# A first layer's preparation put in another order: grouped bias units and a convolution shared by two engines

## The chip, the cores and the metric

The kernel runs on one core of a Trainium2 chip. The metric is the device time of one execution in microseconds; several executions are made and their median is compared. The profile is one execution, read by engine: PE is TensorE (PEld its weight loads), DVE is VectorE, ACT is ScalarE, POOL is GpSimd, SP is the engine that issues most loads. All data are fp32.

## The reference, cut to what matters

The program is a chain of layers. Only the first, a convolutional attention with offsets learned from the queries, is touched:

```python
xn = bn(x)                                        # x: (2, 128, 32, 32)
q = gconv1x1(xn, qw)                              # 8 groups of 16 channels
off = conv(q by group, off_dw_w, stride 4, pad 1) # depthwise 6x6, output 8x8
off = tanh(off_pw_w . gelu(off + b)) * 4          # two offsets for each of 64 keys
vgrid = (grid + off) scaled to [-1, 1]
kv = grid_sample(xn by group, vgrid)              # bilinear
k, v = gconv1x1(kv, kw), gconv1x1(kv, vw)
pos = grid_q[:, :, None] - vgrid[:, None]         # 1024 queries x 64 keys x (x, y)
bias = sign(pos) * log1p(abs(pos))
bias = relu(bias @ cpb_w1 + cpb_b1)               # 2 -> 32
bias = relu(bias @ cpb_w2 + cpb_b2)               # 32 -> 32
bias = bias @ cpb_w3 + cpb_b3
attn = softmax(q k^T * scale + bias);  out = attn v
```

Since pos is a difference along x and one along y, the first bias layer is a sum of a part that depends on the query's column (A) and one that depends on its row (B). After the first layer come two more attention layers, a trajectory network, a gated linear attention and experts; they are the same in both kernels.

## The kernel before

`l0_bias` (L222) runs one block of all engines: `l0_prepare` (L235) and behind it `l0_scores` (L517). Each engine has its own program, in the written order, and engines meet only at semaphores, so an instruction that waits holds all behind it on its engine. PSUM has eight banks of 128x512 fp32.

`l0_prepare` goes through these steps. x is normalised in two halves, the first by VectorE (L289), the second by ScalarE (L351). Four projections by TensorE give the queries (L418), which ScalarE puts into an image with a border (`qpad`, L356) and VectorE copies flat (L296). The depthwise convolution is 36 products of TensorE with diagonal weights that VectorE builds (`TAP`, L292), each over every fourth pixel (L424). Gelu (L359), a product (L432) and Tanh (L362) give the offsets; TensorE meanwhile transposes the image (L438) and ScalarE evicts it (`XT`, L365). VectorE turns offsets into positions (L300 to L306): `spread` feeds a product with ones that gives every sampling point's coordinates (L447), and `pos` goes through Abs, Sign and Ln on ScalarE (L374 to L377) and becomes `F` (L308) and its negative `NF` (L309).

Then come 16 bias units, one for each image and head, of which each is two matmuls of 32 rows (L467, one for A, one for B), and each pair of banks is evicted by VectorE, the last few in part by ScalarE (L315, L322, L392, L399). Between them stand eight sampling steps: ScalarE makes a hat function in two operations (L383, L386), POOL multiplies it with the other axis' (`wt`, L280) and TensorE sums (L476). Keys and values follow (L492, L493), then their spreading by head (`vm`, `KM`) and eight transposes (L499).

`l0_scores` first multiplies B by the second layer (`offsets`, L644), evicts that as `NEGC` by both engines (L559, L589), computes `constants` (L654, L592) and then runs 64 cycles. In a cycle half of the hidden units go POOL (row sum, L553), ScalarE (relu, L567), TensorE (L673), ScalarE (L573), TensorE (L711); the other half go VectorE (a maximum of A and of a negated B, `max1`, L605), TensorE (L673), VectorE (`max2`, L613), TensorE (L720). The negated B for `max1` is a product of `NF` (`negb`, L666), made once for four cycles; every four cycles a tile of scores is evicted (L620) and a query-key product opens the next (L701).

SP loads the packed weights of the layer in two parts and the next stage's behind them (L2557, L2558, L2546); x is loaded by ScalarE's queue (L348).

Of the kernel before, what the change touches and what calls it, by code (L numbers as in the profile page):

```python
# [19 lines left out]
P = 128  # L20
NB = 2
# [125 lines left out]
def l0_pack(w):  # L147
# [37 lines left out]
    p.add("tmask", (rows[:, None] % 4 == np.arange(4)).astype(np.float32))  # L185
# [5 lines left out]
    p.add("qgrid", np.tile(cq.reshape(1, HW), (P, 1)))  # L191
# [16 lines left out]
UNITS = NB * HEADS  # L208
LOOPED = 12
WITH_SAMPLE = (2, 1, 2, 1, 1, 1, 1, 1)  # L210
A_ON_ACT = (11, 12, 13, 14, 15)
B_ON_ACT = (14, 15)


def unit(u):

    return u % NB, u // NB


def evicted(on_act, u, act):  # L220

    return sum((k in on_act) == act for k in range(u + 1))  # L222


def l0_bias(nc, X, PS, W, first, rest, loads, KM, VT, Q, A, WORK, NF, SALL, x_in, x_dram):
# [12 lines left out]
def l0_prepare(st, block, X, PS, W, first, rest, KM, VT, Q, A, WORK, NF, x_in, x_dram):
    sb, sem = st.sb, st.sem
    B = WORK[:, 0:NB * PAIRS * PIX].rearrange("p (r n i x) -> p r n i x", r=2, n=NB * PAIRS, i=4)  # L240
    SPARE = WORK[:, NB * PAIRS * PIX:]
# [4 lines left out]
    TAP = part(4096, TAPS * P).rearrange("p (t o) -> p t o", o=P)  # L246
    qpad = part(9216, NB * PADW * PADW).rearrange("p (b y x) -> p b y x", b=NB, x=PADW)
# [15 lines left out]
    F = sb("l0_f", [P, HALF])  # L263

    inner = lambda b, y0, n: qpad[:, b, 1 + y0:1 + y0 + n, 1:1 + HW]
    flat2 = lambda v: v.rearrange("p a n -> p (a n)")
    CONV, ZED, GRID_X, GRID_Y, SAMPLE, KVB = 4, 5, 6, 4, 6, 7
    
    

    @block.gpsimd
    def _(pool):
        pool.memset(qpad[:], 0.0).then_inc(sem("border"), 1)
        pool.memset(ones[:], 1.0).then_inc(sem("ones"), 1)
        pool.wait_ge(sem("hx"), 1)
        for c in range(8):
            pool.wait_ge(sem("hy"), c + 1)
            if c >= 2:
                pool.wait_ge(sem("sampled"), c - 1)
            pool.tensor_tensor(wt[:, c % 2], hx[:], hy[:, c % 2], ALU.mult).then_inc(sem("wt"), 1)  # L280

    @block.vector
    def _(dve):
        link = Chain(dve, sem("dve_chain"))
        dve.wait_ge(first, 16)
        link(dve.tensor_scalar(s1[:], W["bn1_g"], BN_SCALE, None, ALU.mult))
        dve.sem_inc(sem("s1"), 1)
        dve.wait_ge(x_in[0], 16)
        dve.tensor_scalar(XN[:, 0:PIX], X[:, 0:PIX], s1[:, 0:1], W["bn1_b"], ALU.mult, ALU.add).then_inc(sem("xn0"), 1)  # L289
        for h in range(2):  # L290
            t = slice(h * TAPS // 2, (h + 1) * TAPS // 2)
            dve.tensor_tensor(TAP[:, t], bc(W["ident"], 1, TAPS // 2), bc(W["off_dw_w"][:, t], 2, P), ALU.mult  # L292
                              ).then_inc(sem("taps"), 1)
        for n in range(NCH):
            dve.wait_ge(sem("q_in"), n + 1)
            dve.tensor_copy(Q[:, n * CH:(n + 1) * CH], PS[:, n]).then_inc(sem("q_flat"), 1)  # L296

        dve.wait_ge(rest, 16)
        dve.wait_ge(sem("tanh"), 1)
        link(dve.scalar_tensor_tensor(V[:], V[:], 4.0, W["kgrid"], ALU.mult, ALU.add))  # L300
        link(dve.tensor_scalar(V[:], V[:], 2.0 / 7.0, -1.0, ALU.mult, ALU.add))
        link(dve.tensor_scalar(px[:], V[:], 1.0, HW / 2.0, ALU.add, ALU.mult))
        dve.tensor_tensor(spread[:], bc(px[:], 1, HEADS), bc(W["first"], 2, KEYS), ALU.mult).then_inc(sem("spread"), 1)
        link(dve.tensor_tensor(sel[:], V[:].rearrange("p (t k) -> p t k", t=4), bc(W["tmask"], 2, 16), ALU.mult))
        link(dve.tensor_reduce(own[:], sel[:].rearrange("p t k -> p k t"), AX.X, ALU.add))
        dve.tensor_tensor(pos[:], bc(W["qgrid"], 1, 16), bc(own[:], 2, HW), ALU.subtract).then_inc(sem("pos"), 1)  # L306
        dve.wait_ge(sem("logs"), 1)
        dve.tensor_tensor(F[:], sgn[:], mag[:], ALU.mult).then_inc(sem("f"), 1)  # L308
        dve.scalar_tensor_tensor(NF[:], sgn[:], -1.0, mag[:], ALU.mult, ALU.mult)  # L309

        def a_out(u):
            b, g = unit(u)
            n = b * HEADS + g
            dve.wait_ge(sem("ab"), u + 1)
            dve.tensor_scalar(A[:, n // 2, (n % 2) * 16:(n % 2) * 16 + 16].rearrange("p u q -> p (u q)"),  # L315
                              PS[:, 2 * b], W["cpb_b1"], None, ALU.add).then_inc(sem("a_dve"), 1)

        def b_out(u):
            b, g = unit(u)
            n = b * HEADS + g  # L320
            dve.wait_ge(sem("ab"), u + 1)
            dve.tensor_copy(B[:, :, n // 2, 2 * (n % 2):2 * (n % 2) + 2].rearrange("p r i x -> p i r x"),  # L322
                            PS[:, 2 * b + 1].rearrange("p (i r x) -> p i r x", i=2, r=2)).then_inc(sem("b_dve"), 1)

        for u in range(LOOPED):
            if u not in A_ON_ACT:
                a_out(u)
            b_out(u)
        dve.wait_ge(sem("sampled"), 8)
        got = PS[:, SAMPLE:SAMPLE + NB, 0:P].rearrange("p b (g k) -> p b g k", g=2)  # L330
        link(dve.tensor_scalar(kv[:], got[:, :, 0], W["pmask"][:, 0:1], None, ALU.mult))
        dve.scalar_tensor_tensor(kv[:], got[:, :, 1], W["pmask"][:, 1:2], kv[:], ALU.mult, ALU.add).then_inc(sem("kv"), 1)
        b_out(LOOPED)
        dve.wait_ge(sem("k"), 1)
        for b in range(NB):
            m = bc(W["gmask"], 2, KEYS)
            dve.tensor_tensor(vm[:, b], bc(PS[:, KVB, NB * KEYS + b * KEYS:NB * KEYS + (b + 1) * KEYS], 1, HEADS), m,
                              ALU.mult).then_inc(sem("vm"), 1)
        for b in range(NB):
            m = bc(W["gmask"], 2, KEYS)  # L340
            dve.scalar_tensor_tensor(KM[:, b], bc(PS[:, KVB, b * KEYS:(b + 1) * KEYS], 1, HEADS), DH ** -0.5, m,
                                     ALU.mult, ALU.mult).then_inc(sem("km"), 1)
        b_out(LOOPED + 1)

    @block.scalar
    def _(act):
        for b in range(NB):
            act.dma_start(X[:, b * PIX:(b + 1) * PIX], x_dram[b].rearrange("c h w -> c (h w)")).then_inc(x_in[b], 16)  # L348
        act.wait_ge(sem("s1"), 1)
        act.wait_ge(x_in[1], 16)  # L350
        act.activation(XN[:, PIX:T], X[:, PIX:T], ACT.Identity, bias=W["bn1_b"], scale=s1[:, 0:1]  # L351
                       ).then_inc(sem("xn1"), 1)
        act.wait_ge(sem("border"), 1)
        for n in range(NCH):
            act.wait_ge(sem("q"), n + 1)
            act.activation(inner(n // 2, 16 * (n % 2), 16), PS[:, n].rearrange("p (y x) -> p y x", x=HW),  # L356
                           ACT.Copy).then_inc(sem("q_in"), 1)
        act.wait_ge(sem("conv"), 1)
        act.activation(off[:].rearrange("p b k -> p (b k)"), PS[:, CONV, 0:NB * KEYS], ACT.Gelu,  # L359
# [3 lines left out]
        for n in range(4):  # L363
            act.wait_ge(sem("xt"), n + 1)
            act.activation(XT[:, 4 * n:4 * n + 4].rearrange("p c k -> p (c k)"), PS[:, n],  # L365
                           ACT.Copy).then_inc(sem("xt_out"), 1)
        act.wait_ge(rest, 16)
        act.wait_ge(sem("grid"), 1)
        act.activation(hy[:, 0], flat2(PS[:, GRID_X:GRID_X + 2]), ACT.Abs, bias=W["minus_x"]).then_inc(sem("ax"), 1)
        act.wait_ge(sem("ax"), 1)  # L370
        act.activation(hx[:], hy[:, 0], ACT.Relu, bias=1.0, scale=-1.0).then_inc(sem("hx"), 1)
# [5 lines left out]
        act.activation(mag[:], mag[:], ACT.Ln, bias=1.0).then_inc(sem("logs"), 1)  # L377
        act.wait_ge(sem("hx"), 1)

        def hat(c):  # L380
            if c >= 2:
                act.wait_ge(sem("wt"), c - 1)
            act.activation(hy[:, c % 2], flat2(PS[:, GRID_Y:GRID_Y + 2]), ACT.Abs, bias=W["minus_y"][:, c:c + 1]  # L383
                           ).then_inc(sem("ay"), 1)
            act.wait_ge(sem("ay"), c + 1)
            act.activation(hy[:, c % 2], hy[:, c % 2], ACT.Relu, bias=1.0, scale=-1.0).then_inc(sem("hy"), 1)  # L386

        def a_out(u):
            b, g = unit(u)
            n = b * HEADS + g  # L390
            act.wait_ge(sem("ab"), u + 1)
            act.activation(A[:, n // 2, (n % 2) * 16:(n % 2) * 16 + 16].rearrange("p u q -> p (u q)"),  # L392
                           PS[:, 2 * b], ACT.Identity, bias=W["cpb_b1"]).then_inc(sem("a_act"), 1)

        def b_out(u):
            b, g = unit(u)
            n = b * HEADS + g
            act.wait_ge(sem("ab"), u + 1)
            act.activation(B[:, :, n // 2, 2 * (n % 2):2 * (n % 2) + 2].rearrange("p r i x -> p i r x"),  # L399
                           PS[:, 2 * b + 1].rearrange("p (i r x) -> p i r x", i=2, r=2), ACT.Copy  # L400
                           ).then_inc(sem("b_act"), 1)

        for c in range(8):
            hat(c)
        for u in range(LOOPED - 1, UNITS):
            a_out(u)
            if u in B_ON_ACT:
                b_out(u)
# [2236 lines left out]
```

## Time and profile before

| what | us |
|---|---|
| median of 3 runs (1671.84 to 1678.54) | 1673.09 |
| profiled execution, its own time | 1676.29 |
| its span, first to last instruction | 1674.4 |
| PE busy / DVE busy / ACT busy / POOL busy | 1500.5 / 886.2 / 872.5 / 320.8 |
| first product of the score loop, from the span's start | 89.90 |
| mean granted TensorE clock over the span | 0.955 |

A timeline row gives the start, the duration, the engine, the line, the operation, what it writes and reads, the shapes and the count; in brackets stands how long the engine had been idle and who released it. A row with a count is several instructions merged. The granted clock is a share of the full 2.4 GHz; its two levels are 1.0 and 0.5. The column holds 1.00 until the first recorded change.

### The profile page before, as it was taken

To read this page: it belongs to the slowest core of one execution; us is meant where nothing else is said; L and a number is where in the kernel's file an instruction comes from. 1 tells how busy PE (TensorE), PEld (TensorE's weight loads), DVE (VectorE), ACT (ScalarE), POOL (GpSimd) and SP (SyncE) were. 2 spreads that over 40 slices of the span, in tenths; PEclk is the share of its full clock that TensorE was granted. 3 is DMA by queue.
4 is the path that set the end of the run, shared out by engine and by line. 5 is a ranking of instruction groups with operands and counts; after the bars stand their busy time and mean duration, and the time that the engine had idled before them with its cause. 6 is when DMAs were issued, how large, how long until landed. Compare 5 with 4: busy or idle time off the path is not lost. (4 is left out here: it accounts for less than half of the span.)

```text
span 1674.4 us, 29793 instructions
## 1 busy us (share of the span) xinstructions
PE 1500.5 (90%) x12334; PEld 739.5 (44%) x12334; DVE 886.2 (53%) x1364; ACT 872.5 (52%) x1292; POOL 320.8 (19%) x139
## 2 busy tenths in 40 slices
PE   6889999999778997999999999899999999939678
PEld 4322222222243774666666666554444444316333
DVE  2578888888772554677777777110002000258243
ACT  3567777777543435677777776232222222250451
POOL 0746666666220001000000000000000000020000
PEclk9589999999998999799999999899999999979899
DMA  1000000000001003444344431000000000000000
GB/s 65 1 2 2 2 2 2 2 2 2 2 22 77 0 1 118 147 150 162 134 173 177 165 151 39 1 1 0 1 0 0 0 0 0 31 0 4 1 1 25
DMA packets 21089, 69.66 MB, mean 42 GB/s; under 512 B 736, under 2 KB 17248, under 8 KB 18656
## 3 DMA queue, kind: packets, MB, share of 16 engines
q1 hardware_dynamic: 20672, 66.76, 10.7%
q8 instruction: 96, 1.57, 0.4%
q10 hardware_dynamic: 288, 1.05, 0.2%
q14 instruction: 33, 0.27, 0.1%
HBM read 33.21 MB, written 34.60 MB: 40 GB/s over the span
## 5 line engine op out<-in xcount | busy, mean ns | idle before, releaser
L553 POOL TENSOR_TENSOR l_work<-l_a_scores,l_work 128x2048 f32<-128x2048 f32 x64 | 232.9, 3640 | 126.5 <-PE banks L673 126.5
L1909 PE MATMUL banks<-s_h,pack_l2f_l3f 128*128 128x512 f32 x512 | 221.0, 592 | 0.0
L1938 ACT ACTIVATE s_h<-banks,pack_l2f_l3f 128x512 f32<-128x512 f32 x128 | 88.0, 688 | 239.2 <-PE banks L1909 175.7
L1510 ACT ACTIVATE r_e<-banks,r_max 128x512 f32<-128x512 f32 x256 | 162.1, 685 | 51.2 <-DVE r_max L1551 51.1
L613 DVE TENSOR_TENSOR l_work<-banks,sc_negc 128x1024 f32<-128x1024 f32 x128 | 156.2, 1221 | 49.6 <-PE banks L720 33.2
L573 ACT ACTIVATE l_work<-banks,pack_l 128x1024 f32<-128x1024 f32 x128 | 142.7, 1115 | 74.7 <-PE banks L673 73.7
L673 PE MATMUL banks<-l_work,pack_l 32*32 32x512 f32 x4096 | 159.6, 606 | 23.5 <-ACT l_work L573 19.8
L1545 DVE TENSOR_REDUCE r_raw<-banks 128x1 f32<-128x640 f32 (+1 forms) x128 | 109.8, 858 | 90.6 <-PE banks L1435 88.9
L1455 PE MATMUL banks<-pack_l2a,r_e 128*128 128x128 f32 x1024 | 147.5, 285 | 10.4 <-ACT r_e L1510 10.2
L1909 PEld LDWEIGHTS banks<-s_h,pack_l2f_l3f 128*128 128x128 f32 x512 | 97.3, 190 | 122.5 <-issue 122.5
L1435 PE MATMUL banks<-r_k,r_q 32*128 32x128 f32 (+3 forms) x832 | 148.8, 466 | 1.1 <-DVE r_v L1379 1.1
L605 DVE TENSOR_TENSOR l_work<-banks,l_a_scores 128x2048 f32<-128x2048 f32 x64 | 146.0, 2281 | 0.7 <-PE banks L666 0.7
L567 ACT ACTIVATE l_work<-l_work 128x1024 f32<-128x1024 f32 x128 | 134.3, 1052 | 9.6 <-POOL l_work L553 9.6
L1455 PEld LDWEIGHTS banks<-pack_l2a,r_e 128*128 128x128 f32 x1024 | 112.0, 142 | 54.7 <-ACT r_e L1510 46.1
L1964 DVE TENSOR_SCALAR s_k<-banks,pack_l2f_l3f 128x512 f32<-128x512 f32 x12 | 9.0, 750 | 221.8 <-PE banks L1914 221.8
L1435 PEld LDWEIGHTS banks<-r_k,r_q 32*128 32x128 f32 x832 | 87.4, 188 | 71.7 <-issue 55.0
L673 PEld LDWEIGHTS banks<-l_work,pack_l 32*32 32x32 f32 x4096 | 42.1, 103 | 138.2 <-issue 103.3
L2136 POOL MEMSET ga_keep<- 128x1024 f32 x1 | 1.0, 951 | 474.0 <-SPq L2067 474.0
L1559 DVE COPY r_pt<-banks 128x512 f32<-128x512 f32 x128 | 87.9, 687 | 4.1 <-PE banks L1455 3.5
L1518 ACT ACTIVATE r_pt<-banks 128x512 f32<-128x512 f32 x128 | 76.5, 597 | 25.1 <-PE banks L1455 25.1
L1420 PE MATMUL banks<-pack_l2a,r_q 32*128 32x257 f32 x224 | 80.1, 437 | 0.0
L1551 DVE CUSTOM_DVE_ANT_0 banks<-banks,r_band,r_raw 128x384 f32<-128x384 f32 (+1 forms) x128 | 75.9, 593 | 6.3 <-DVE r_raw L1545 0.2
(399 smaller groups left out, 2079.1 us busy)
## 6 DMA issues: line engine op xcount, KB each, us to landing
distances<-r_rd SPq DMA_DIRECT2D x16, 2048.0 KB, 6.5
r_band<-distances SPq DMA_DIRECT2D x16, 1536.0 KB, 7.0
pack_l2f_l3f<-pack_dram_l2f SPq DMA_DIRECT2D x1, 2244.5 KB, 10.4
pack_l2f_l3f<-pack_dram_l3f SPq DMA_DIRECT2D x1, 1248.5 KB, 7.0
residual<-x ACTq DMA_DIRECT2D x2, 512.0 KB, 6.1
out<-residual SPq DMA_DIRECT2D x4, 256.0 KB, 2.0
pack_l<-pack_dram_l SPq DMA_DIRECT2D x1, 945.0 KB, 7.5
pack_l2a<-pack_dram_l2a SPq DMA_DIRECT2D x1, 715.0 KB, 5.5
```

The costliest lines, as they stand in the source:

```text
L553: pool.tensor_tensor(image(H1R[:, (c + 1) % 3]), bc(a, 2, 16), bc(b, 3, HW), ALU.add).then_inc(sem("added"), 1)
L567: act.activation(h, h, ACT.Relu).then_inc(sem("relu"), 1)
L573: act.activation(H2R[:, (2 * c + part) % 3], PS[:, RELU:RELU + 2], ACT.Relu, bias=W["cpb_b2"]).then_inc(sem("h2_relu"), 1)
L605: dve.tensor_tensor(image(H1M[:, c % 2]), bc(b, 3, HW), bc(a, 2, 16), ALU.max).then_inc(sem("h1_max"), 1)
L613: dve.tensor_tensor(image(H2M[:, (2 * c + part) % 3]), image(PS[:, MAX + j:MAX + j + 2]), bc(NEGC[:, j:j + 2, n, i, rows(half)], 3, HW), A ...
L673: ins = pe.matmul(PS[32 * u:32 * u + 32, bank], w2(j), h[32 * j:32 * j + 32, u], start=True, stop=True, tile_position=(32 * j, 32 * u))
L1435: ins = pe.matmul(PS[:, 2 * (t % 2) + a, col:col + n * P], Qm[at, a, h % 2, b * PIX + t * P:b * PIX + (t + 1) * P], K[at, a, b, slot:slot ...
L1455: ins = pe.transpose(PS[:, 4 + h, j * P:(j + 1) * P], E[:, t % 2, c:c + P], W["ident"])
L1510: act.activation(E[:, t % 2, a * CH:(a + 1) * CH], PS[:, 2 * (t % 2) + a], ACT.Exp, bias=mx[:, t % 2:t % 2 + 1], scale=-1.0).then_inc(sem( ...
L1545: dve.tensor_reduce(raw[:, one], v[:, lo:hi], AX.X, ALU.min).then_inc(sem("far"), 1)
L1909: ins = pe.matmul(bank, W["w2"][:, col:col + P], H1[:, c, m], start=(m == 0), stop=(m == HB - 1))
L1938: act.activation(H[:, c, k], PS[:, g % 8], ACT.Tanh, bias=bias).then_inc(sem("tanh"), 1)
```

## The change

The preparation is written anew; the score loop keeps its order with small edits.

- Loads: SP waits for x before it sends the second part of the weights and the next stage's.
- Both halves of x are normalised by VectorE. TensorE starts with five products on a constant that nobody reads. The first half of the transposes moves ahead of the convolution.
- The convolution is split: 12 taps stay on TensorE, 24 go to VectorE in two alternating accumulators, whose sum a last product of TensorE with the identity adds. The bordered image has another layout, so that a tap is one access pattern.
- `pos` comes before `spread`; the table for Ln is loaded explicitly behind Tanh; Abs, Sign and Ln come before the sampling coordinates on ScalarE. TensorE waits for `hx` before the first unit.
- The signs of the y rows of half the keys are folded into `tmask` and `qgrid`, so `NF` is gone.
- The 16 units become eight groups: four matmuls on all four row groups, into banks 0 to 3. VectorE evicts both images' A in one instruction, ScalarE both images' B. A group waits for both evictions of the one before.
- Sampling: three of eight weights stay on ScalarE and POOL, five are made by VectorE from ScalarE's distance. The order is written out. The sampled sums share bank 6 or 7 with keys and values.
- The first row sum on POOL moves between its second and third product.
- The offsets' products and the evictions to `NEGC` (halved, by image) move into the preparation, between keys and values. `constants` moves into the first cycle of the loop; `negb` serves eight cycles instead of four.

```diff
-    p.add("tmask", (rows[:, None] % 4 == np.arange(4)).astype(np.float32))
+    turned = (rows[:, None] >= P // 2) & (np.arange(16) // 4 % 2 == 1)
+    sign = np.where(turned, np.float32(-1.0), np.float32(1.0))
+    p.add("tmask", (rows[:, None] % 4 == np.arange(4)).astype(np.float32)[:, :, None] * sign[:, None, :])
...
+PE_TAPS = 12
+ON_POOL = (0, 2, 4)
+ON_DVE = (1, 3, 5, 7, 6)
+UNIT_ORDER = ("u0", "u1", "s1", "u2", "s0", "u3", "s3", "u4", "s2", "u5", "s5", "u6", "s4", "u7", "s7", "s6")
...
     @block.gpsimd
...
+        for c in ON_POOL:
+            pool.wait_ge(sem("hat"), c // 2 + 1)
+            if c:
+                pool.wait_ge(sem("sampled"), SAMPLE_ORDER.index(c - 2) + 1)
+            pool.tensor_tensor(wt[:, 0], hx[:], hy[:, 0], ALU.mult).then_inc(sem("wt_pool"), 1)
+            if c == 2:
...
+                rows_sum(pool, A, B, H1R, 0).then_inc(sem("added"), 1)
     @block.vector
...
+        dve.wait_ge(sem("q_in"), NCH)
+        for t in range(PE_TAPS, TAPS):
+            k, n = t % 2, (t - PE_TAPS) // 2
...
+            if n:
+                dve.wait_ge(chain, n)
+                ins = dve.scalar_tensor_tensor(ACCS[:, k], tap(t), weight, ACCS[:, k], ALU.mult, ALU.add)
+            else:
+                ins = dve.tensor_scalar(ACCS[:, k], tap(t), weight, None, ALU.mult)
+            ins.then_inc(chain, 1)
...
+        def a_out(g):
+            dve.wait_ge(sem("ab"), g + 1)
+            n, t = g // 2, g % 2 * 16
+            dve.tensor_scalar(A[:, n::PAIRS, t:t + 16].rearrange("p b u x -> p b (u x)"), PS[:, 0:NB], W["cpb_b1"], None,
+                              ALU.add).then_inc(sem("a"), 1)
+        def weights(c):
...
+            dve.tensor_scalar(wt[:, slot], hy[:, slot], -1.0, 1.0, ALU.mult, ALU.add).then_inc(sem("near"), 1)
...
+            dve.scalar_tensor_tensor(wt[:, slot], wt[:, slot], 0.0, hx[:], ALU.max, ALU.mult).then_inc(sem("wt_dve"), 1)
+        for k in range(4):
+            a_out(2 * k)
+            weights(2 * k + 1)
+            a_out(2 * k + 1)
+        weights(6)
...
     @block.scalar
...
+        act.preload_act_table_set("natural_log_exp_and_others")
...
+        for k in range(4):
+            distance(2 * k + 1)
+            b_out(2 * k)
+            distance(2 * k)
+            if 2 * k in ON_POOL:
+                hat(2 * k)
+            b_out(2 * k + 1)
...
     @block.tensor
...
+        pe.wait_ge(sem("busy"), 1)
+        for _ in range(5):
+            keep_clock(busy[:, 0:P], busy)
...
+        for t in range(PE_TAPS):
+            pe.matmul(PS[:, CONV, 0:NB * KEYS], TAP[:, t], tap(t), start=(t == 0), stop=False)
+        pe.wait_ge(sem("conv_dve"), 1)
...
+        pe.wait_ge(sem("hx"), 1)
+        def units(g):
+            if g == 0:
+                pe.wait_ge(sem("f"), 1)
+                pe.wait_ge(sem("xt_dve"), 2)
+            else:
+                pe.wait_ge(sem("a"), g)
+                pe.wait_ge(sem("b"), g)
             for c in range(2):
...
+                for b in range(NB):
+                    r = 32 * (NB * c + b)
...
+                    ins = pe.matmul(PS[:, NB * c + b], W["cpb_w1"][r:r + 32, g * P:(g + 1) * P], f, start=True, stop=True,
+                                    tile_position=(r, 0))
...
+        row_offsets(pe, PS, W, B, 0).then_inc(sem("c"), 1)
         pe.wait_ge(sem("kv"), 1)
...
+        row_offsets(pe, PS, W, B, 1).then_inc(sem("c"), 1)
...
 def l0_scores
...
+            if c == 0:
+                constants()
+            if c % 8 == 7 and c + 1 < CYCLES:
+                negb((c + 1) // 8)
...
             def load_l0(sp):
                 sp.dma_start(tile[:, 0:split], packs["l0"][:, 0:split]).then_inc(arrived["l0"], 16)
+                for b in range(NB):
+                    sp.wait_ge(x_in[b], 16)
                 sp.dma_start(tile[:, split:], packs["l0"][:, split:]).then_inc(rest, 16)
```

## Rows read from the trace of the kernel before

**Rows 1.** Stages: stretch, length, busy us (count) by engine, clock, DMA share, GB/s.

```profile
32.62:42.62 10.00, 3.36 (x33) 2.26 (x33) 3.14 (x9) 8.56 (x13) 0.00 (x0) 0.79 0.01 2
42.62:80.12 37.50, 34.05 (x196) 12.68 (x196) 20.33 (x33) 19.50 (x21) 29.51 (x11) 0.55 0.00 0
80.12:89.90 9.78, 7.57 (x109) 4.21 (x108) 2.78 (x2) 7.29 (x9) 0.00 (x0) 0.86 0.01 3
89.90:118.74 28.84, 25.25 (x367) 6.14 (x382) 21.82 (x14) 18.58 (x19) 14.56 (x4) 0.82 0.01 2
```

**Rows 2.** Timeline up to 35 us: start, duration, engine, line, operation, count, [idle, releaser].

```profile
5.17 0.81 DVE L289 TENSOR_SCALAR l_work<-residual,l_s,pack_l 128x1024 f32<-128x1024 f32 x1 [0.15 <-DMA residual<-x]
...
5.90 5.02 DVE L292 TENSOR_TENSOR l_work<-pack_l 128x2304 f32<-128x2304 f32 x2
...
8.99 1.28 ACT L351 ACT_TABLE_LOAD   x1 [8.99 <-DMA residual<-x]
...
11.57 3.47 PE L418 MATMUL banks<-l_work,pack_l 128*128 128x512 f32 x4 [1.76 <-ACT l_work L351]
...
15.73 16.89 PE L424 MATMUL banks<-l_work 128*128 128x128 f32 x72 [0.69 <-ACT l_work L356]
...
33.42 1.97 PE L438 MATMUL banks<-pack_l,l_work 128*128 128x128 f32 x16
```

**Rows 3.** Timeline from the convolution's end to the first units.

```profile
33.89 0.23 DVE L300 SCALAR_TENSOR_TENSOR l_v<-l_v,pack_l 128x64 f32<-128x64 f32 x1 [17.48 <-ACT l_v L362]
...
35.40 1.14 PE L447 MATMUL banks<-l_spread,l_ones 32*128 32x512 f32 x8
...
35.77 0.69 DVE L306 TENSOR_TENSOR l_pos<-pack_l,l_own 128x512 f32<-128x512 f32 x1
...
41.21 0.63 ACT L377 ACTIVATE l_mag<-l_mag 128x512 f32<-128x512 f32 x1
...
42.62 2.09 PE L467 MATMUL banks<-l_f,pack_l 32*128 32x512 f32 x8 [6.08 <-DVE l_f L308]
```

**Rows 4.** Timeline in the unit stage and at the offsets.

```profile
44.74 0.75 DVE L315 TENSOR_SCALAR l_a_scores<-banks,pack_l 128x512 f32<-128x512 f32 x1 [1.57 <-PE banks L467]
...
50.51 2.08 PE L467 MATMUL banks<-l_f,pack_l 32*128 32x512 f32 x4
...
52.52 1.08 PE L476 MATMUL banks<-l_wt,l_work 128*32 128x128 f32 x16
...
53.13 1.11 ACT L383 ACTIVATE l_hy<-banks,pack_l 128x1024 f32<-128x1024 f32 x1 [2.15 <-POOL l_wt L280]
...
53.78 2.35 POOL L280 TENSOR_TENSOR l_wt<-l_hx,l_hy 128x1024 f32<-128x1024 f32 x1 [0.68 <-PE banks L476]
...
82.02 2.75 PE L644 MATMUL banks<-l_work,pack_l 32*32 32x512 f32 x64
```

**Rows 5.** Timeline in the score loop, at its entry and around one L666.

```profile
100.63 2.28 DVE L605 TENSOR_TENSOR l_work<-banks,l_a_scores 128x2048 f32<-128x2048 f32 x1
...
108.21 2.28 DVE L605 TENSOR_TENSOR l_work<-banks,l_a_scores 128x2048 f32<-128x2048 f32 x1
...
118.74 2.28 DVE L605 TENSOR_TENSOR l_work<-banks,l_a_scores 128x2048 f32<-128x2048 f32 x1
...
238.81 2.28 DVE L605 TENSOR_TENSOR l_work<-banks,l_a_scores 128x2048 f32<-128x2048 f32 x1
...
242.35 1.12 PE L666 MATMUL banks<-l_nf,pack_l 32*128 32x256 f32 x4
...
243.66 2.28 DVE L605 TENSOR_TENSOR l_work<-banks,l_a_scores 128x2048 f32<-128x2048 f32 x1
...
245.64 3.64 POOL L553 TENSOR_TENSOR l_work<-l_a_scores,l_work 128x2048 f32<-128x2048 f32 x1 [2.19 <-PE banks L673]
...
246.69 1.23 DVE L613 TENSOR_TENSOR l_work<-banks,sc_negc 128x1024 f32<-128x1024 f32 x1 [0.75 <-PE banks L720]
...
249.40 2.28 DVE L605 TENSOR_TENSOR l_work<-banks,l_a_scores 128x2048 f32<-128x2048 f32 x1
```

More of the change, by code:

```diff
@@ L205, in mlp_pack, with l0_bias @@
     return p
[L208 to L225, printed above, removed]
+PE_TAPS = 12
+ON_POOL = (0, 2, 4)
+ON_DVE = (1, 3, 5, 7, 6)
+CYCLES = NB * PAIRS * 2 * 4
+RING = NB * PAIRS * 4 * P
+UNIT_ORDER = ("u0", "u1", "s1", "u2", "s0", "u3", "s3", "u4", "s2", "u5", "s5", "u6", "s4", "u7", "s7", "s6")
+SAMPLE_ORDER = tuple(int(x[1]) for x in UNIT_ORDER if x[0] == "s")
+def l0_bias(nc, X, PS, W, first, rest, loads, KM, VT, Q, A, WORK, F, SALL, x_in, x_dram):
     with ExitStack() as ctx:
         st = Stage(nc, ctx)
+        NEGC = st.sb("sc_negc", [P, 4, NB * PAIRS, 4, HW])
+        negb2 = st.sb("sc_negb2", [P, 1])
         block = st.block()
@@ L303, in _ @@
         dve.tensor_tensor(spread[:], bc(px[:], 1, HEADS), bc(W["first"], 2, KEYS), ALU.mult).then_inc(sem("spread"), 1)
-        link(dve.tensor_tensor(sel[:], V[:].rearrange("p (t k) -> p t k", t=4), bc(W["tmask"], 2, 16), ALU.mult))
-        link(dve.tensor_reduce(own[:], sel[:].rearrange("p t k -> p k t"), AX.X, ALU.add))
-        dve.tensor_tensor(pos[:], bc(W["qgrid"], 1, 16), bc(own[:], 2, HW), ALU.subtract).then_inc(sem("pos"), 1)
+        for n in range(2, 4):
+            dve.wait_ge(sem("xt"), n + 1)
+            dve.tensor_copy(turned(n), PS[:, XT_BANK[n]]).then_inc(sem("xt_dve"), 1)
@@ L388, in a_out @@
[L388 to L408, printed above, removed]
+        act.wait_ge(rest, 16)
+        act.wait_ge(sem("grid"), 1)
+        act.activation(hy[:, 0], flat2(PS[:, GRID_X:GRID_X + 2]), ACT.Abs, bias=W["minus_x"]).then_inc(sem("ax"), 1)
+        act.wait_ge(sem("ax"), 1)
+        act.activation(hx[:], hy[:, 0], ACT.Relu, bias=1.0, scale=-1.0).then_inc(sem("hx"), 1)
+        act.wait_ge(sem("hx"), 1)
@@ new lines, in distance @@
+        def distance(c):
+            slot = c % 2
+            if slot and c >= 3:
+                act.wait_ge(sem("near"), ON_DVE.index(c - 2) + 1)
+            elif c >= 2:
+                act.wait_ge(sem("wt_pool"), c // 2)
+            act.activation(hy[:, slot], flat2(PS[:, GRID_Y:GRID_Y + 2]), ACT.Abs, bias=W["minus_y"][:, c:c + 1]
+                           ).then_inc(sem("far_odd" if slot else "far_even"), 1)
+        def hat(c):
+            act.wait_ge(sem("far_even"), c // 2 + 1)
+            act.activation(hy[:, 0], hy[:, 0], ACT.Relu, bias=1.0, scale=-1.0).then_inc(sem("hat"), 1)
@@ L666, in negb @@
                 ins = pe.matmul(PS[:, NEGB, low * 256:low * 256 + 256], W["cpb_w1"][r:r + 32, k * P:(k + 1) * P],
-                                NF[r:r + 32].rearrange("p (k y) -> p k y", y=HW)[:, :, rows(half)], start=True,
+                                F[r:r + 32].rearrange("p (i r x) -> p i r x", i=2, r=2)[:, :, 1], start=True,
                                 stop=True, tile_position=(r, 0), skip_group_check=True)
@@ L744, in _, with reg_wait @@
         layer3_max(CYCLES - 1)
+def reg_wait(eng, sem, value, passed):
+    eng.wait_ge(sem, value)
+    eng.sem_inc(passed, 1)
 def l0_attend(nc, X, PS, W, SALL, VT, loads):
```

346 lines of the change are left out of this document (161 added, 185 removed).

## The prediction

> **What bounds the kernel now.** I read the stage table first: the first layer's preparation, from the start to the first product of the score loop at 89.90 us, is the only part that the diff touches, with the score loop behind it. Its stages [rows 1] come strictly one after another, each released by the last instruction of the one before, so every microsecond taken out of one of them moves the whole rest of the program forward. Then I read the timeline inside each stage. Until 32.62 TensorE is the chain: 72 passes of the depthwise convolution take 16.89 us, 0.235 us each, after the second half of the image had been waited for until 8.99 [rows 2]. From 32.62 to 42.62 a chain of small operations crosses all engines, with ScalarE busy 8.56 of 10.00 us [rows 1]. From 42.62 to 80.12 sixteen bias units alternate with eight sampling steps: each unit takes 2.08 us on TensorE, each sampling step 1.08, and the evictions lie between them [rows 4]; the granted clock there is 0.55 of full, mostly the 1.2 GHz level [rows 1]. In the loop a cycle is 4.85 us (start of one L605 to the next), and 5.74 where the product L666 stands in it [rows 5].
>
> **The change, step by step.** The sum is made against the profiled execution: span 1674.4, its time 1676.29 us, 3.2 above the median of 1673.09.
>
> Step 1, up to the end of the convolution (now 32.62). VectorE normalises both halves (0.81 us each) instead of leaving the second to ScalarE, which waited until 8.99 and then loaded a table (1.28) [rows 2]. SP now holds its two large loads until x is in, so x has less beside it. I put the first normalised half at 5.2 and the second before it is needed. The four projections cost 1.73 us each by the trace (3.47 for two [rows 2]); the eight passes of L447 take 1.14 and the same packing in L467 takes 2.09 after the clock has fallen [rows 3], so 1.73 is the price at the low level whatever the clock's column says there, and at the high one it is about 0.9. The five unread products at the start begin as soon as a memset is done; I take two projections at either price: 5.2 + 2 x 1.73 + 2 x 0.9 = 10.4, and 0.69 for the last eviction, the wait that the convolution's row shows [rows 2]: 11.1. Bounds 9.8 (all fast; then ScalarE's table load and evictions end last) and 12.8 (all slow). Then 24 taps run on VectorE and 12 on TensorE (24 passes x 0.235 = 5.6 us, hidden behind them; without that cover nothing grows until it passes the taps). No row shows a 128x128 tap; a 128x64 operation takes 0.23 [rows 3] and a 128x512 one 0.69 [rows 3], so about 0.27 by interpolation: 24 x 0.27 = 6.5, then 0.3 for the sum of the two accumulators and 0.5 for the identity's two passes. End at 18.4 instead of 32.62: **-14.2** (bounds 16.1 to 22.7, with taps at 0.23 and 0.38).
>
> The upper tap price comes from a row: passes over strided pixels take 0.235 us, transposes of as many contiguous columns 0.123 (1.97 for 16) [rows 2]; the excess, 0.11, put on each tap gives 0.38. The Trainium skill, page "SBUF — State Buffer", section "Door 1: The DMA port swizzle", says that fp32 read with steps of four elements leaves a 16-byte line at every access and pays for it. By that rule the taps, which have the same step, would be slow too and the sum 2.7 us worse; the trace agrees for TensorE, and no run shows it for VectorE.
>
> The loads held on SP cost nothing: 'rest' is first needed at the convolution's end; even if it took a whole 9 us [rows 2] after x it would be there by about 15. If it were not, both VectorE and TensorE would stand.
>
> Step 2, to the first unit (now 10.00 us). Gelu, shift and tanh are unchanged: 1.27 to the first VectorE step (33.89 [rows 3]). Then V, its scaling, the masked product and the reduction (4 x 0.25), pos 0.69, px 0.23, spread 0.69, grid product 1.14 [rows 3], and two ScalarE steps of 1.1, for TensorE now waits for hx before the first unit: 7.4, with hand-overs 7.7. The logarithm's path ends at 1.27 + 1.0 + 0.69 + 3 x 0.63 + 0.69 = 5.6 and is hidden behind it; its table load is now ahead of pos, in ScalarE's idle time. **-2.3** (bounds -1.5 and -2.7).
>
> Step 3, first unit to the loop's first product (now 37.50 + 9.78 = 47.28). Four matmuls on all four row groups go together: eight passes took 2.09, four 2.08 [rows 3, 4], so eight groups cost what eight single units did. But the banks are single: a group waits for both evictions of the one before. Eviction of 128x1024 by VectorE: 1.23 to 1.28 (0.75 for 512 columns plus 0.53; 1.23 in a loop row [rows 4, 5]). Group period 2.09 + 1.28 + 0.18 of hand-overs = 3.55; seven periods 24.9. The sampling product (1.08) fits in the gap. Engines by themselves: ScalarE 19 steps of 1.1 = 20.9, VectorE 8 x 1.28 + 5 x (0.81 + 1.23) = 20.4, POOL 3 x 2.35 + 3.64 = 10.7, all under 28. POOL's first row sum stands between its second and third product; the step behind it is needed at about 30 us after the convolution and ready at 29, so its 3.64 is covered, by one microsecond. Tail: last unit, its eviction, the last weights and sampling product 2.09 + 1.28 + 2.04 + 1.08 + 0.2 = 6.7; first offsets 2.0 (64 passes took 2.75 over both clock levels [rows 4]), their eviction 1.3, key and value products with the steps around them 2.1, second offsets 2.0, evictions, transposes and two relus 4.4: 11.8. Sum 43.4 at 1.2 GHz: **-3.9**. At the full clock a group is 1.14 (the same packing, earlier [rows 3]) + 1.28 + 0.2 = 2.62 and the tail 1 shorter: about 35.8, -11.5.
>
> Step 4, the loop's entry, first product to its sixth L605 (now 28.84 at a mean clock of 0.82 [rows 1, 5]). One product L666 less (0.9), and the evictions of the offsets no longer stand directly before it; but the constants now lie inside the first cycle (about 2 us). I take 26: **-2.8**, bounds 23 (clock high throughout) and 29.
>
> Step 5, the rest of the loop. L666 now serves eight cycles, not four. One occurrence lengthens a cycle from 4.85 to 5.74, and TensorE, not VectorE, is then late (0.75 of waiting behind it) [rows 5]: seven more times 0.89, **-6.2** (bounds 0 and -7).
>
> The negated positions' separate tensor, the folded signs and the smaller moves lie beside work that ends later: 0.
>
> Sum: -14.2 - 2.3 - 3.9 - 2.8 - 6.2 = -29.4. From 1676.3 that is 1646.9; from the median **1644**, with 1637 to 1651 as its own range.
>
> **The rivals.**
> *The clock is high in the units.* In the trace it fell before the first unit, and stayed down while two of four row groups worked at a time [rows 1]. Now all four work, which speaks for a rise; the gap of about 1.4 us after each group, of which sampling fills 1.08, and the wait for hx ahead of the first unit speak against it. Price: 7.6 us better, 1636; part of the stage gives part of it.
> *Slow taps and slow projections.* Both upper bounds of step 1, 4.3 us worse: 1648.
> *VectorE is locked out by POOL.* While a POOL product (2.35) or row sum (3.64 [rows 4, 5]) runs, the new weights on VectorE, which read one or two SBUF tensors, could stand; those five steps lie between the evictions that free the banks. Followed through the order above, one collision near the row sum and one or two near the products lengthen the chain by 1.6 to 3.6: 1646 to 1648. The Trainium skill, "SBUF — State Buffer", section "SBUF: two separate sides", has this rule: the shared port pair goes to one of VectorE and GpSimd for a whole instruction. No row before shows it: VectorE there reads PSUM while POOL works.
> *Slower.* The score loop starts cold and stays so. A cycle at the low clock took 7.58 (100.63 to 108.21 [rows 5]) against about 5.4 on average: 2.2 us a cycle. From the 14th cold cycle on the gain of 29.4 is gone; with all 64 cold it is 141 - 29 us on the wrong side, 1785. Against it: the loop before also starts partly cold and comes up by itself within the entry [rows 1].
> *The gain of step 5 does not come*, since VectorE takes over as the late one: 6.2 worse, 1650.
>
> **How the numbers follow.** Chances: forecast 0.55, high clock 0.20, slow step 1 0.10, lock-out 0.08, no gain in step 5 0.04, cold loop 0.03. The range 1632 to 1655 takes in the first five with their bounds. 0.5% (8.4 us) is about what a measurement of this kernel can tell from no change; only the cold loop, or several bad bounds at once, come to that: faster 0.95, same 0.02, slower 0.03.
>
> **What would show it.** Step 1: the Gelu at 18.4, taps of 0.27. Step 2: first unit 7.7 later. Step 3: groups 3.5 apart with 2.1 on TensorE and a clock of 0.5; 2.6 apart would be the high clock, irregular gaps before VectorE's weights the lock-out. Step 5: L605 every 4.85 at the cycles that had 5.74. The prediction is wrong if the Gelu comes after 23, if groups are more than 4 us apart, or if the loop's clock stays at 0.5 past its first cycles.

## The result and the profile after

| | before | after |
|---|---|---|
| median | 1673.49 (4 runs) | 1652.13 (4 runs, 1647.80 to 1656.02) |
| ratio, 95% interval | | 0.986 [0.9839, 0.9881] |
| profiled execution, its own time | 1676.29 | 1647.80 |
| its span | 1674.4 | 1646.0 |
| start of the last maximum of the score loop | 434.57 | 408.94 |
| span behind that | 1239.8 | 1237.1 |

The change saves 21.4 us, 1.4%. That is 8 us less than the forecast; the median lies inside its wide range, 1632 to 1655, and just outside the narrow one, 1637 to 1651.

The steps of the prediction, each between the same two events in the two profiled executions:

| step | forecast | in the profile after |
|---|---|---|
| 1, to the convolution's end | 18.4, -14.2 | 20.53, -12.1 |
| 2, to the first unit | 7.7, -2.3 | 8.48, -1.5 |
| 3, to the loop's first product | 43.4, -3.9 | 43.82, -3.5 |
| 4, to the sixth maximum | 26, -2.8 | 26.75, -2.1 |
| 5, sixth to last maximum | -6.2 | 309.36 where it was 315.83, -6.5 |
| behind, same code | 0 | -2.7 |

The five steps give -25.7, where -29.4 was forecast: 3.7 us were sized too well. Against its own profiled execution the forecast was 1646.9, and this one took 1647.80, since another 2.7 came in behind the loop. The rest lies between profiled executions and medians: that of before was 2.8 above the median of its four runs, this one is 4.3 below its own.

Steps 3 to 5 are read between the sixth and the last maximum before (118.74 in [rows 5] and the first row here) and the loop's first product, sixth and last maximum after (the other three):

```profile
434.57 2.28 DVE L605 TENSOR_TENSOR l_work<-banks,l_a_scores 128x2048 f32<-128x2048 f32 x1
```

```profile
72.83 2.57 PE L712 MATMUL banks<-l_work,pack_l 32*32 32x512 f32 x32 [2.13 <-ACT l_work L617]
...
99.58 2.28 DVE L648 TENSOR_TENSOR l_work<-banks,l_a_scores 128x2048 f32<-128x2048 f32 x1
...
408.94 2.28 DVE L648 TENSOR_TENSOR l_work<-banks,l_a_scores 128x2048 f32<-128x2048 f32 x1
```

The timeline from the first input to the sampling coordinates is next (columns as in [rows 2]). L334 is the normalisation of a half of x, L496 the four projections, L417 ScalarE's evictions into the bordered image, L346 and L344 VectorE's 24 taps, L502 TensorE's 12, L504 the product with the identity, L487 the two halves of the transposes, L524 the coordinates.

```profile
5.25 0.81 DVE L334 TENSOR_SCALAR l_work<-residual,l_s,pack_l 128x1024 f32<-128x1024 f32 x1 [0.41 <-DMA residual<-x]
...
6.12 4.25 PE L496 MATMUL banks<-l_work,pack_l 128*128 128x512 f32 x8 [0.30 <-DVE l_work L334]
...
7.88 1.28 ACT L417 ACT_TABLE_LOAD   x1 [7.88 <-PE banks L496]
...
9.17 2.10 ACT L417 ACTIVATE l_work<-banks 128x512 f32<-128x512 f32 x4
...
10.20 1.04 PE L487 MATMUL banks<-pack_l,l_work 128*128 128x128 f32 x8
...
11.30 0.58 DVE L346 TENSOR_SCALAR l_work<-l_work,pack_l 128x128 f32<-128x128 f32 x2 [2.40 <-ACT l_work L417]
...
11.41 5.77 PE L502 MATMUL banks<-l_work 128*128 128x128 f32 x24 [0.17 <-ACT l_work L417]
11.79 7.80 DVE L344 SCALAR_TENSOR_TENSOR l_work<-l_work,pack_l 128x128 f32<-128x128 f32 x22
...
20.04 0.49 PE L504 MATMUL banks<-l_work,pack_l 128*128 128x128 f32 x2 [2.86 <-DVE l_work L350]
20.57 0.37 ACT L425 ACTIVATE l_off<-banks,pack_l 128x128 f32<-128x128 f32 x1 [5.07 <-PE banks L504]
...
21.45 1.97 PE L487 MATMUL banks<-pack_l,l_work 128*128 128x128 f32 x8
...
24.55 2.09 PE L524 MATMUL banks<-l_spread,l_ones 32*128 32x512 f32 x8 [1.13 <-DVE l_spread L362]
```

The taps begin at 11.30, where the forecast had 11.1. They take 8.29 us (11.30 to 19.59), 0.35 each, where it had 0.27. TensorE is done after 5.77 us and then waits 2.86 for VectorE. The same eight transposes take 1.04 ahead of that wait and 1.97 behind it, and L524 takes 2.09, as the same packing did late in before [rows 3], instead of the 1.14 that step 2 counted. The table by stretch (columns as in [rows 1], the clock third from the end) has the reason: the clock falls to the 1.2 GHz level 0.9 us behind the wait's end. In the profiles of four other runs with this wait it fell between 0.8 us ahead of its end and 0.7 behind.

```profile
18.00:20.00 2.00, 0.00 (x0) 0.00 (x0) 1.90 (x7) 0.00 (x0) 0.00 (x0) 1.00 0.00 0
20.00:21.00 1.00, 0.49 (x2) 0.30 (x2) 0.05 (x1) 0.37 (x1) 0.00 (x0) 0.95 0.00 0
21.00:22.00 1.00, 0.92 (x11) 0.78 (x12) 0.17 (x1) 0.40 (x2) 0.00 (x0) 0.50 0.00 0
```

The rows below are the unit stage around its sixth and seventh group (L543). L372 is VectorE's eviction, L380 and L383 the two operations of its weights, L318 the weights' product on POOL, L253 the row sum.

```profile
43.67 3.63 POOL L253 TENSOR_TENSOR l_work<-l_a_scores,l_work 128x2048 f32<-128x2048 f32 x1
...
45.04 2.81 DVE L380 TENSOR_SCALAR l_wt<-l_hy 128x1024 f32<-128x1024 f32 x1
...
45.18 1.14 PE L543 MATMUL banks<-l_f,pack_l 32*128 32x512 f32 x8 [0.77 <-DVE l_a_scores L372]
...
47.26 2.79 POOL L318 TENSOR_TENSOR l_wt<-l_hx,l_hy 128x1024 f32<-128x1024 f32 x1
...
47.96 3.17 DVE L383 SCALAR_TENSOR_TENSOR l_wt<-l_wt,l_hx 128x1024 f32<-128x1024 f32 x1
50.01 4.61 POOL L253 TENSOR_TENSOR l_work<-l_a_scores,l_work 128x2048 f32<-128x2048 f32 x1
51.05 1.27 DVE L372 TENSOR_SCALAR l_a_scores<-banks,pack_l 128x1024 f32<-128x1024 f32 x1
...
52.38 2.09 PE L543 MATMUL banks<-l_f,pack_l 32*128 32x512 f32 x8
...
55.74 0.68 DVE L380 TENSOR_SCALAR l_wt<-l_hy 128x1024 f32<-128x1024 f32 x1
...
56.52 1.23 DVE L383 SCALAR_TENSOR_TENSOR l_wt<-l_wt,l_hx 128x1024 f32<-128x1024 f32 x1
```

Undisturbed, L380 takes 0.68 and L383 1.23 (the last two rows); here they take 2.81 and 3.17. Read the ends: L253 ends at 47.30 and L380 0.55 behind it, at 47.85; L318 ends at 50.05 and L383 1.08 behind it, at 51.13. The one that came second ended 0.55 and 1.08 us behind the first, close to what it takes undisturbed: it did its work only once the other had ended. POOL's L318 and second L253 are longer by about what VectorE held, 2.79 for 2.35 and 4.61 for 3.63. The eviction that frees the banks (51.05) stands behind L383, so the groups are 7.20 apart, against 3.50 at the low clock (29.01 to 32.51) and 2.55 to 3.13 at the high one. TensorE waits 4.87 us in this stall (46.32 to 51.19), and the granted clock falls in it: it is 1.00 up to 48.00, 0.61 from there to 49.00, and 0.50 when the seventh group runs at 2.09.

### The profile page after: what moved, and what is told of

It reads as the page before. It is cut to its first block and busy times, and to the rows that moved or that the text cites. A ratio compares the mean times of both kernels' runs of the same rounds, so it can differ in the third digit from the quotient of the medians.

```text
span 1646.0 us, 29662 instructions
## 1 busy us (share of the span) xinstructions
PE 1466.8 (89%) x12266; PEld 720.1 (44%) x12266; DVE 895.9 (54%) x1381; ACT 868.4 (53%) x1289; POOL 310.8 (19%) x134
## 5 line engine op out<-in xcount | busy, mean ns | idle before, releaser
L253 POOL TENSOR_TENSOR l_work<-l_a_scores,l_work 128x2048 f32<-128x2048 f32 x64 | 233.9, 3654 | 122.1 <-PE banks L712 115.0
```

Source lines behind the costliest of these rows:

```text
L253: return pool.tensor_tensor(image(H1R[:, (c + 1) % 3]), bc(A[:, n, 8 * i:8 * i + 4], 2, 16), bc(b, 3, HW), ALU.add)
```

## Experiments

All of them change the kernel after; ratios are to the kernel before on the same chip. First that kernel once more, as a partner (run after_again):

> The changed kernel once more, for its spread and a second profile. If the whole gain lies in the first layer, the last L648 of the score loop stands about 25.6 us earlier than in the kernel before (408.9 in the first profile) and what is left of the span behind it differs only by the clock of later stages: median between 1648 and 1654, spans that differ by some 6 us although the first layer's end differs by less than 2. If instead the first layer itself varies, its end varies as much as the span.

Measured: 1651.60 (1649.18 to 1658.45), ratio 0.9855 [0.9832, 0.9878]. Its last maximum stands at 410.12, 24.5 us ahead of the kernel before. Its profile has the same picture: taps of 0.35, L380 2.39 and L383 3.18, and 6.8 us between the same two groups.

### What makes a tap 0.35 us

```diff
-        return qpad[:, y % 4, y // 4 + 1:y // 4 + 9, :, x:x + 29:4]
+        return qpad[:, y % 4, y // 4 + 1:y // 4 + 9, :, x:x + 8]
```

> Every tap, on TensorE and on VectorE, reads eight neighbouring pixels in place of every fourth (so the convolution's values are others). If the step of four elements is the price: passes on TensorE fall from 0.235 to about 0.12, taps on VectorE from 0.35 to 0.27-0.29, and Gelu comes 1.5 to 2 us earlier than 20.2. Rival: VectorE's 0.35 is the fixed price of an operation with two SBUF inputs and a wait on its own semaphore; then only TensorE's passes shrink, and Gelu stays within 0.3, since VectorE ends last.

Every tap here reads eight neighbouring pixels in place of every fourth, so it is another convolution, of the same size. Groups by line and form; between the bars stand the busy time in us and the mean of one in ns: first the kernel after, then this one.

```profile
L344 DVE SCALAR_TENSOR_TENSOR l_work<-l_work,pack_l 128x128 f32<-128x128 f32 x22 | 7.8, 448 | 0.0
L502 PE MATMUL banks<-l_work 128*128 128x128 f32 x24 | 5.8, 412 | 0.2 <-ACT l_work L417 0.2
```

```profile
L344 DVE SCALAR_TENSOR_TENSOR l_work<-l_work,pack_l 128x128 f32<-128x128 f32 x22 | 5.9, 346 | 0.0
L502 PE MATMUL banks<-l_work 128*128 128x128 f32 x24 | 3.1, 285 | 0.2 <-ACT l_work L417 0.2
```

A mean is the time from an instruction's start to its end, and they overlap; the step from one to the next is the busy time over the count. It is 0.355 us on VectorE with the stride and 0.266 without, and 0.240 against 0.129 for a pass of TensorE. The Gelu comes at 18.62 instead of 20.20 to 20.57. So the stride costs both engines about as much for each pass, 0.09 and 0.11 us, and without it the interpolated 0.27 holds. The kernel's one time is 1643.94.

### Does POOL hold VectorE?

Three products of ones by ones on POOL, whose result nobody reads, beside the taps (run pool_in_conv):

```diff
+        pool.wait_ge(sem("ones"), 1)
+        pool.wait_ge(sem("q_in"), NCH)
+        for k in range(3):
+            pool.tensor_tensor(wt[:, 1].rearrange("p (n k) -> p n k", k=P), bc(ones[:], 1, GCOLS // P),
+                               bc(ones[:], 1, GCOLS // P), ALU.mult).then_inc(sem("extra"), 1)
+            pool.wait_ge(sem("extra"), k + 1)
...
+        dve.wait_ge(sem("extra"), 3)
```

> Three extra POOL products of 128x1024 (of ones, read by nobody), one after another, while VectorE works on its taps; nothing else is changed. Theory lock-out: each holds the ports for about 2.3 us, taps show durations of 1 to 2.5 instead of 0.35, and Gelu comes 3 to 7 us later than 20.2. Rival (POOL does not disturb VectorE; the long operations of the unit stage had another cause): all taps 0.35, Gelu within 0.5.

In this run L352 and L350 are VectorE's taps, L509 TensorE's, and L316 the extra products.

```profile
10.61 2.23 DVE L352 TENSOR_SCALAR l_work<-l_work,pack_l 128x128 f32<-128x128 f32 x2 [1.87 <-ACT l_work L424]
10.72 5.77 PE L509 MATMUL banks<-l_work 128*128 128x128 f32 x24 [0.17 <-ACT l_work L424]
10.73 5.93 POOL L316 TENSOR_TENSOR l_wt<-l_ones 128x1024 f32<-128x1024 f32 x3 [7.48 <-ACT l_work L424]
12.76 11.01 DVE L350 SCALAR_TENSOR_TENSOR l_work<-l_work,pack_l 128x128 f32<-128x128 f32 x22
```

The 24 taps take 13.2 us instead of 8.3: of POOL's 5.9, 4.9 are added to VectorE, and the Gelu comes at 25.05. TensorE reads the same image at the same time and stays at 5.77. The lock-out between VectorE and POOL is thereby shown by itself. The kernel's one time is 1657.80.

### What the lock-out costs in the units

The row sum is put behind VectorE's last weights (run rows_late):

```diff
-            if c == 2:
-                pool.wait_ge(sem("conv"), 1)
...
-                rows_sum(pool, A, B, H1R, 0).then_inc(sem("added"), 1)
+        pool.wait_ge(sem("wt_dve"), len(ON_DVE))
+        pool.wait_ge(sem("conv"), 1)
...
+        rows_sum(pool, A, B, H1R, 0).then_inc(sem("added"), 1)
```

> The first row sum of POOL is put behind the last of VectorE's five weights, as are all that follow it; nothing else is changed. Theory lock-out: the long operations of VectorE in the unit stage (2.81 instead of 0.68, 3.17 instead of 1.23) stood behind a POOL operation on the same memory ports. Then no weights operation is longer than 1.3 except beside a POOL product, the distance of group 5 to group 6 falls from 7.2 to 3.5 or less, the loop's first product comes 3 to 5 us earlier and the median falls by 2 to 4. Rival clock: these durations follow TensorE's clock level; the distance stays above 6 and the time within 1.

```profile
43.80 0.68 DVE L380 TENSOR_SCALAR l_wt<-l_hy 128x1024 f32<-128x1024 f32 x1
43.93 1.14 PE L543 MATMUL banks<-l_f,pack_l 32*128 32x512 f32 x8 [0.76 <-DVE l_a_scores L372]
44.58 1.23 DVE L383 SCALAR_TENSOR_TENSOR l_wt<-l_wt,l_hx 128x1024 f32<-128x1024 f32 x1
...
47.06 1.14 PE L543 MATMUL banks<-l_f,pack_l 32*128 32x512 f32 x8 [0.55 <-DVE l_a_scores L372]
...
65.49 2.92 PE L712 MATMUL banks<-l_work,pack_l 32*32 32x512 f32 x32 [1.50 <-ACT l_work L617]
```

Both operations are back at 0.68 and 1.23, the two groups are 3.13 apart, and the loop's first product comes at 65.49, 8.1 earlier than in its partner's profile (73.62). Part of that is the clock, which rose two groups earlier here. A cleaner partner is the run that makes `negb` every four cycles (two sections below; its edit acts only in the loop), whose first six groups start within 0.02 us of these. It has the lock-out:

```profile
43.95 1.14 PE L543 MATMUL banks<-l_f,pack_l 32*128 32x512 f32 x8 [0.76 <-DVE l_a_scores L372]
...
51.16 2.09 PE L543 MATMUL banks<-l_f,pack_l 32*128 32x512 f32 x8
...
72.09 3.02 PE L712 MATMUL banks<-l_work,pack_l 32*32 32x512 f32 x32 [1.36 <-ACT l_work L617]
```

The two groups are 7.21 apart, the groups behind take 2.09 instead of 1.14, and the first product comes at 72.09. So a stall of 4.1 us was followed by another 2.5 us, with TensorE at the low clock. The last maximum stands at 402.27, 7.9 ahead of the partner's. In the median, though, the run is 1650.43, ratio 0.9844 [0.9823, 0.9865], 1.2 us under its partner, with intervals that overlap: by itself the gain is not shown in the time. The stretch behind the last maximum, the same code in all kernels, lay between 1234.8 and 1247.1 in the twelve profiles, and that scatter covers it.

### The unread products, and the clock

```diff
                 units(int(what[1]))
+                keep_clock(W["ident"], F[:, 0:2 * P])
```

> One unread 128x128 by 128x256 product on TensorE behind each group of bias units, the thing that the change leaves out. Theory clock: the granted clock is 1.0 from the second or third group to the last, all groups take 1.14 instead of 2.09, and the stage is 3 to 5 us shorter, the median lower by as much. Theory lock-out: the two long VectorE operations stay, the distance of group 5 to 6 stays at 6 or more, and the median moves by less than 2, since a group also waits for evictions of 1.28 and the extra product itself takes 0.43 to 0.85.

Measured: 1650.59 (1645.67 to 1659.95), ratio 0.9837 [0.9807, 0.9867]. L380 and L383 still take 2.82 and 3.18, the groups are 7.2 apart, and the first product comes at 73.48 against 73.62. The product ran at 46.27, and still the group at 52.41 took 2.09. While VectorE stands, it doesn't help.

### Step 5, and the split of the convolution

```diff
-            if c % 8 == 7 and c + 1 < CYCLES:
-                negb((c + 1) // 8)
+            if c % 4 == 3 and c + 1 < CYCLES:
+                negb((c + 1) // 4)
```

> The negated positions' product is made for every four cycles again, as before; the rest as in the changed kernel. Step 5: eight more products of 0.89 on the path, seven of them behind the sixth maximum: distance from there to the last maximum 309.4 + 6.2 = 315.6, and the median 6 to 7 higher than the changed kernel's. Rival: the gain came from elsewhere in the loop; then the distance stays at 309.4 within 1.

Measured: 316.16 us from the sixth to the last maximum, against 309.36 and 309.82; median 1659.23, ratio 0.9902 [0.9884, 0.992], 7 to 8 us slower than the two measurements of the kernel after. Seven extra products thus cost 0.9 to 1.0 each, and step 5 stands.

All 36 taps on TensorE, without VectorE's taps and the identity's product:

```diff
-PE_TAPS = 12
+PE_TAPS = 36
...
-        dve.tensor_tensor(ACCS[:, 0], ACCS[:, 0], ACCS[:, 1], ALU.add).then_inc(sem("conv_dve"), 1)
```

> All 36 taps on TensorE again, in the new layout, no taps on VectorE; the rest as in the changed kernel. By step 1 the convolution is 72 passes of 0.235 = 16.9 us from 11.3 on, Gelu at 28.5 instead of 20.6: 7.9 us later, and the median higher by as much. Rival: TensorE's clock does not fall at 21 any more, because it is not idle behind its own taps, so that the grid's product takes 1.14 instead of 2.09 and the first groups run fast: only 4 to 6 us.

The Gelu came at 29.08, 8.9 later than the partner's, of which 1.35 is a wait for the diagonal weights, since VectorE must build 36 there and not 12 (the convolution begins at 12.10 instead of 10.75). The last maximum came at 417.25, 7.1 later. Part of the rival held: the clock stayed high behind the convolution, and the coordinates' product took 1.45 instead of 2.09. The median is 1654.81, ratio 0.986 [0.9837, 0.9883]: only 3.2 above the partner, inside the scatter again, while the profile of the stage is clear.

### Both faults mended

VectorE's taps are dearer than counted and TensorE waits 2.86 us for them, so four go back to TensorE, with the row sum late as in rows_late (run late_16; late_16_again and late_16_kept are the two behind it):

```diff
-PE_TAPS = 12
+PE_TAPS = 16
```

> Row sums behind the last weights, as in rows_late, and 16 taps on TensorE with 20 on VectorE: 32 passes x 0.235 = 7.5 against 20 x 0.35 = 7.0, so both end together, and Gelu comes 0.7 us earlier than 20.2. The last maximum of the loop at 401.5 where rows_late had 402.3; the median 1 to 2 below rows_late if the clock of later stages does not hide it.

Measured: 1645.08 (1640.62 to 1653.72), ratio 0.9808 [0.979, 0.9826]. Once more, and with the unread products:

> The kernel of late_16 once more (row sums behind VectorE's last weights, 16 taps on TensorE), as the partner on the same chip for the next run. Theory (the first layer is shorter by the lock-out and one microsecond of taps, later stages only scatter): last max1 between 396 and 405 us in the profile, by whether the clock is high in the units, and a median between 1640 and 1647. Rival (late_16's 1645 was chance, the edit is worth nothing): median 1650 to 1652 as the changed kernel had.

> late_16_again with an unread product of 128x128 by 128x256 of TensorE behind each group of bias units. Nothing holds VectorE there now, so the clock decides the stage: at 1.2 GHz a group was 2.09 and 3.50 apart from the next, at 2.4 GHz 1.14 and 2.55. Theory (without the lock-out the unread product keeps or raises the clock): all groups but the first two at 1.14, first unit to the loop's first product 36 to 38 us against 36.8 to 42.6 without it, so median 2 to 5 us under its partner. Rival (the clock in the units falls and rises independently of it, or the product, 0.4 to 0.6 us, only fills time in front of the next group): same stage as its partner within 2 us, or groups later by up to 0.5 each, median the same or up to 3 us more.

Measured: 1645.94, ratio 0.9809 [0.9782, 0.9836], and with the products 1647.03, ratio 0.9813 [0.9788, 0.9838]. Two runs agree on some 32 us under the kernel before and about 6 under the second measurement of the kernel after; the products add nothing. Which of the two edits gave how much, the medians don't show. Where 401.5 was forecast for the last maximum, against 402.27 in rows_late, the two profiles have 404.77 and 403.07, since the units ran longer at the low clock. The convolution's part differs from the forecast of the first run, which gave the 16 taps 0.7 us (late_16_again, from the convolution on; the last row by itself is from the first run):

```profile
10.74 7.63 PE L502 MATMUL banks<-l_work 128*128 128x128 f32 x32 [0.18 <-ACT l_work L417]
18.18 0.40 PE L504 MATMUL banks<-l_work,pack_l 128*128 128x128 f32 x2
...
19.39 1.09 PE L487 MATMUL banks<-pack_l,l_work 128*128 128x128 f32 x8
22.48 2.09 PE L524 MATMUL banks<-l_spread,l_ones 32*128 32x512 f32 x8 [2.00 <-DVE l_spread L362]
```

```profile
23.08 1.14 PE L524 MATMUL banks<-l_spread,l_ones 32*128 32x512 f32 x8 [2.00 <-DVE l_spread L362]
```

TensorE waits for nothing before L504 now, and the clock stays high through the second transposes: 1.09, not 1.97, and L504 takes 0.40, not 0.49 to 0.80. The Gelu is at 19.22 in the first and 18.62 in the other two profiles. Part of that is where the taps begin, which varies from 10.6 to 11.3; from the first tap on it comes after 8.0 us, where the two profiles of the kernel after had 9.27 and 9.56. So 1.3 to 1.6 were won, about VectorE's time for four taps. For the coordinates' product (L524) the gain didn't last: TensorE waits 2.00 us for `spread` ahead of it, and it took 1.14 in the first profile and 2.09 in the other two.

In the units the clock went its own way. The first profile ran all eight groups at 2.09, 3.50 apart, and took 42.56 us from the first to the loop's first product (26.59 to 69.15); the second had five groups at 1.14 and took 39.56; with the unread products it was 37.75. The products gained 1.8 us in that stage against their partner and nothing by the loop's last maximum: 402.79 against 403.07.

## Why the prediction was right or wrong

**Step 1** was wrong in one term, the price of a tap. The number was interpolated between two contiguous operations [rows 3]; a strided pass of TensorE lay in the rows with a higher one [rows 2], was used as the upper bound, 0.38, and set aside. The measured 0.35 is close to that bound, and taking the stride away gives back 0.266. The rival of slow taps, with 10 in 100, thereby came true in its taps. All else in the step held to 0.2 us, in part by luck. The first half of x was normalised at 6.06, not 5.2; the four projections took 4.25, not 5.3; and what ended last was ScalarE's table load and its four evictions (7.88 to 11.27), a path that the forecast had only in its lower bound. The Trainium skill, page "SBUF — State Buffer", section "Door 1: The DMA port swizzle", states the 16-byte line that the prediction set beside this bound; the runs agree with it on VectorE too, as far as one stride can show; they don't tell a line's price from another price of a stride.

**Step 2** missed 0.8, and L524 alone, at 2.09 instead of 1.14, is 0.95. The forecast took the price of before without asking whether TensorE would be busy ahead of it. Before, all 16 transposes stood directly ahead of this product, with no wait [rows 2, 3]; the change moved half of them away. After, TensorE waited 2.86 us for the late taps, the clock fell, and it waited 1.13 more for `spread`. The late taps are not the whole cause: with them mended (late_16) the product still took 2.09 in two profiles of three, behind a wait of 2.00. Besides, the step's items add to 7.2, not to the 7.4 it gives.

**Step 3** came out at 43.82 for 43.4, and that agreement is an accident. By its own sign the prediction was wrong here: it named groups more than 4 us apart, and two stood 7.20 apart. Two rivals were realised together. The clock was at the high level for four of eight groups, which the forecast didn't have, and the lock-out, which had 8 in 100, took back what that gave. The forecast's own case, low clock and no lock-out, was met in the profile of late_16: 42.56 for 43.4. The high clock without the lock-out, priced at 35.8, was nearly met in rows_late: 36.78, with two groups still at the low level. So the prices were good and the case was wrong. The lock-out was priced at 1.6 to 3.6 and measured 4.1, with 2.5 behind it by the clock, which the rival did not follow. The price also hangs on which operations happen to meet: in pool_in_conv, whose first six groups ran at the low level, the row sum met the same weights later, held L387 (L380 here) for 1.49 instead of 0.68, and the two groups stood 3.93 apart. Beside the rival's low chance stood only that no row of before shows POOL and a VectorE operation on SBUF meeting. That is no evidence that they don't collide. The Trainium skill, "SBUF — State Buffer", section "SBUF: two separate sides", had it right that one of the two engines has the shared ports for a whole instruction: the ends of L253 and L380, and of L318 and L383, show just that.

**Step 4** missed 0.7. The constants' product took 3.64 us at the low clock (0.50 from 75 to 78), where some 2 were counted, and the second maximum came 8.4 us behind the first (71.11 and 79.50).

```profile
75.33 3.64 PE L693 MATMUL banks<-sc_negc,pack_l 128*32 128x256 f32 x32
...
79.50 2.29 DVE L648 TENSOR_TENSOR l_work<-banks,l_a_scores 128x2048 f32<-128x2048 f32 x1
```

**Step 5** was right, -6.5 for -6.2, and the run that undoes it alone gives the same. VectorE did not become late in its place.

**The whole**: 3.7 us too much in the steps, and the rest lies in the scatter of executions. The forecast's own range, 1637 to 1651, had no room for that; the wide one did. The second measurement of the same pair gave -26.3 where the first gave -21.4, and the steps show -25.7.

**Open**: why the clock rises within the units in one execution and not in the next of the same kernel. What was tried, an unread product behind each group, changed the time in neither kernel. Of the steps, the split of the convolution and step 5 were undone by themselves; the grouped units, the unread products at the start, the later loads and the moved offsets were not, so their shares are read from the rows alone.

## What to carry to other kernels

Before work is put on VectorE beside POOL, list for every pair of instructions that can meet whether both work on SBUF, and count the second as starting where the first ends; then follow who waits behind it, TensorE's clock included. Price a strided operation by a strided row, even of another engine, before a contiguous one of the same engine. When work is split between engines, split it so that TensorE is not the one that waits: here four taps moved back took its wait away, won 1.3 to 1.6 us, and kept its clock through the transposes behind them.

## What the runs showed of the hardware

- One VectorE operation of 0.68 us beside a POOL row sum took 2.81, one of 1.23 took 3.17, and POOL's own rose from 3.63 to 4.61. Evictions from PSUM were not held: L372 (43.84) took 1.28 beside the row sum that had begun at 43.67.
- A stride of four fp32 elements cost VectorE 0.09 us on a 128x128 operation (0.355 against 0.266) and TensorE 0.11 on a pass (0.240 against 0.129).
- The granted clock fell within 0.9 us of the end of a 2.86 us wait of TensorE (transposes 1.04 ahead, 1.97 behind it); without that wait it stayed high for them (1.09).
- Behind the score loop, stages with the same code differed by 12 us between profiled executions (1234.8 to 1247.1), which hides an edit of a few microseconds in a median of five; the profile of its stage still shows it.
